# Attention turned by DMA in fp16 halves instead of by TensorE, with the query projection moved into gate/up, in a fused attention and FFN kernel

## The reference

```
xn = layernorm(x)                                   # x: 8 x 1024 x 256
q = elu(xn @ Wq.T) + 1;  k = elu(xn @ Wk.T) + 1;  v = xn @ Wv.T     # 16 heads of 16
kv_state = sum over tokens of k (x) v;  k_state = sum of k          # per batch and head
attn = (q . kv_state) / max(q . k_state, 1e-6)
local = conv over 3 tokens, per channel, of xn, + conv_b
out = x + (attn + local) @ Wp.T + bp + (silu(xn @ wg.T) * (xn @ wu.T)) @ wd.T   # hidden 768
```

## Time and profile before

| | |
|---|---|
| median of 3 runs | 507.55 us (507.19 to 507.74) |
| the profiled execution: its own time | 506.9 us |
| its span, first to last instruction | 505.3 us |
| TensorE matmul busy | 491.4 us, 97% |
| VectorE / ScalarE / GpSimd busy | 430.5 us, 85% / 334.3 us, 66% / 144.7 us, 29% |
| granted TensorE clock | 0.999 of full speed |

### The profile page before, as it was taken

How to read it: one execution, slowest core, us unless ns; L and a number is a source line. 1 busy time by engine, 2 the same in 40 slices (tenths; PEclk the granted TensorE clock), 3 DMA queues, 4 the chain that set the end, 5 groups by cost and what they waited for, 6 DMA issues and landing times.

```text
span 505.3 us, 11017 instructions
## 1 busy us (share of the span) xinstructions
PE 491.4 (97%) x3968; PEld 306.1 (61%) x3968; DVE 430.5 (85%) x833; ACT 334.3 (66%) x522; POOL 144.7 (29%) x152
## 2 busy tenths in 40 slices
PE   7888999999999999999999999999999999999997
PEld 6545364755747566474756657475565756657576
DVE  4889898889888898988889888889888889897786
ACT  2676866667485775757667485667758576674770
POOL 3563415140321405033140502314041141401050
PEclk9999999999999999999999999999999999999999
DMA  8573434333524423252352325233342442233012
GB/s 307 183 91 77 86 82 87 68 111 51 151 43 111 99 45 125 41 166 42 83 125 42 125 42 164 43 82 100 54 138 42 126 82 42 87 50 74 3 42 84
DMA packets 68653, 45.36 MB, mean 90 GB/s; under 512 B 33424, under 2 KB 68112, under 8 KB 68624
## 3 DMA queue, kind: packets, MB, share of 16 engines
q1 hardware_dynamic: 59360, 35.79, 25.2%
q0 software_dynamic: 8448, 8.39, 11.0%
q10 hardware_dynamic: 816, 0.79, 0.5%
HBM read 20.32 MB, written 8.39 MB: 57 GB/s over the span
## 4 chain that ended last, share of the span: by engine, by line
PE 88%; DVE 5%; ACT 3%; DMA 2%; issue 1%; ACTq 0%; DVEq 0%
PE ps L1202 16%; PE ps L1039 16%; PE ps L1211 15%; PE ps L1221 15%; PE ps L1145 15%; PE ps L1101 5%; PE ps L1110 3%; PE ps L1164 2%; DMA wv_raw<-in_L_attn_Wv_dram 2%; DVE maxima L665 1%; DVE hl L902 1%; DVE hid L896 1%; ACT hh L544 1%; DVE cb L764 0%; PE ps L1085 0%
## 5 line engine op out<-in xcount | busy, mean ns | idle before, releaser
L536 ACT ACTIVATE act_g<-ps,scales 128x512 f32<-128x512 f32 x96 | 65.9, 687 | 42.0 <-PE ps L1211 39.7
L896 DVE SCALAR_TENSOR_TENSOR hid<-act_g,scales,ps 128x512 f32<-128x512 f32 x96 | 71.4, 744 | 21.2 <-ACT act_g L536 20.7
L902 DVE TENSOR_TENSOR hl<-hid,hh 128x512 f16<-128x512 f32 x96 | 66.3, 691 | 1.8 <-ACT hh L544 0.4
L361 POOL TENSOR_TENSOR xT<-xh,xl 128x1024 f32<-128x1024 f16 x15 | 32.3, 2153 | 109.4 <-issue 109.4
L544 ACT ACTIVATE hh<-hid 128x512 f16<-128x512 f32 x96 | 59.7, 622 | 5.3 <-DVE hid L896 5.3
L1202 PE MATMUL ps<-xh,g_wh 128*128 128x512 f16 x192 | 57.6, 382 | 2.1 <-ACT u_wh L455 1.4
L1211 PE MATMUL ps<-xl,g_wh 128*128 128x512 f16 x192 | 57.1, 379 | 0.0
L1202 PE MATMUL ps<-xh,u_wh 128*128 128x512 f16 x192 | 57.1, 379 | 0.0
L1211 PE MATMUL ps<-xl,u_wh 128*128 128x512 f16 x192 | 57.1, 379 | 0.0
L1221 PE MATMUL ps<-d_wh,hh 128*128 128x256 f16 x384 | 52.4, 273 | 2.2 <-DVE hid L896 2.2
L499 ACT ACTIVATE k_neg<-ps,scales 128x512 f32<-128x512 f32 x30 | 20.6, 687 | 49.4 <-PE ps L1145 49.4
(11 more groups left out here) (149 smaller groups left out, 965.5 us busy)
## 6 DMA issues: line engine op xcount, KB each, us to landing
xb<-bp_sb SPq DMA_DIRECT2D x16, 512.0 KB, 3.4
xb<-in_L_attn_x_dram POOLq DMA_DIRECT2D x16, 512.0 KB, 5.9
x_in<-in_L_attn_x_dram SPq DMA_DIRECT2D x15, 512.0 KB, 4.1
out_dram<-out_sb SPq DMA_DIRECT2D x14, 512.0 KB, 2.9
out_dram<-out_sb SPq DMA_DIRECT2D x4, 256.0 KB, 2.1
wg_int<-in_L_ffn_w_gate_dram SPq DMA_DIRECT2D x1, 768.0 KB, 7.1
wu_int<-in_L_ffn_w_up_dram SPq DMA_DIRECT2D x1, 768.0 KB, 8.6
wd_int<-in_L_ffn_w_down_dram SPq DMA_DIRECT2D x1, 768.0 KB, 11.1
```

The source lines that it names most:

```text
L536: nc.scalar.activation(act_g[:, j % 2, :], ps[:, gate_bank(j), :], ACT.Silu, scale=silu_in).then_inc(silu_ready, 1)
L896: nc.vector.scalar_tensor_tensor(out=hid[:, j % 2, :], in0=act_g[:, j % 2, :], scalar=h_mul, in1=ps[:, gate_bank(j) + 1, :], op0=ALU.mult, ...
L902: nc.vector.tensor_tensor(hl[:, j, :], hid[:, j % 2, :], hh[:, j, :], ALU.subtract).then_inc(hl_ready, 1)
```

## The change

1. `transpose_attn` is gone from the 14 steps that attend (it stays for the last batch in step (7, 1)). Instead ScalarE writes `attn_h` (fp16, `attn_high(p)`), VectorE writes the rest, `attn_l` (`attn_low(p)`), SP turns each with one DMA transpose (`turn_attn`), GpSimd adds the two into `y` (`begin_y(p)`), and VectorE adds `local` to it (`put_y(p)`, now with both inputs in SBUF).
2. `project_q` moves behind `gate_up(2)`, with `accumulate(1)` behind it, and has banks 4 and 5 for itself; ScalarE evicts both of its parts (`query_evict`, after `silu(2)`; VectorE's `relu_q` is gone), and its exponential (`query_exp`) and `put_q` run in the *next* step.
3. `project_kv(1)` stands before `query`; `project_y(0)` behind `gate_up(5)` and `project_y(1)` between `down(0)` and `down(1)`.
4. On VectorE `stats` comes before the first taps, the second taps go into gate/up, `x_high`/`x_low` move from j = 4 to j = 2, `put_y` to j = 2 and 3, `y_high` to j = 3 and 4, `y_low(0)` to j = 4, `y_low(1)` behind `hidden_low(5)`.
5. In the last step everything of item 1 applies to the attention of batch 6, and `query_evict` and `query_exp` stand before the first `silu`.

The diff, cut to its core:

```
@@ SP
             def turn_attn(b, c):
+                turn([(attn_h, aT_h, attn_h_ready, ah_turned), (attn_l, aT_l, attn_l_ready, al_turned)],
+                     at(b, c, 2, 2), lambda channels: channels[:, :, :, :])
@@ GpSimd
+            def begin_y(b, c, p):
+                pool.wait_ge(ah_turned, at(b, c, 16, 16))
+                pool.wait_ge(al_turned, at(b, c, 16, 16))
+                nc.gpsimd.tensor_tensor(y[:, :, cols].rearrange("p k (i t) -> p i k t", i=2), aT_h[:, tiles, :, :],
+                                        aT_l[:, tiles, :, :], ALU.add).then_inc(y_begun, 1)
...
                     layernorm(nb, ncx)
+                if attend:
+                    begin_y(b - 1, c, 0)
+                    begin_y(b - 1, c, 1)
@@ ScalarE, step
+                    query_exp(*((b, 0) if c == 1 else (b - 1, 1)))
                 key_parts(0)
+                if not ahead:
+                    attn_high(b - 1, c, 0)
                 key_parts(1)
-                if past:
-                    query_parts()
+                if attend and ahead:
+                    attn_high(b - 1, c, 0)
+                if not ahead:
+                    attn_high(b - 1, c, 1)
+                    query_evict()
+                    query_exp(b, c)
@@ VectorE, step
+                if ahead:
+                    stats(nb, ncx)
                 tap(pb, pc, 0, 0)
                 tap(pb, pc, 1, 0)
+                put_q(pb, pc)
+                put_k(0)
...
                         hidden(j)
+                        if attend and j == 0:
+                            attn_low(b - 1, c, 1)
+                        if attend and j == 1:
+                            tap(pb, pc, 0, 2)
+                            tap(pb, pc, 1, 2)
                         if j >= 1:
                             hidden_low(j - 1)
-                        if attend and j == Y_SPLIT[0]:
+                        if attend and j == 4:
                             y_low(b - 1, c, 0)
+                        if attend and j in (2, 3):
+                            put_y(b - 1, c, j - 2)
@@ TensorE, step
+                    project_kv(1)
+                    query(b - 1, c, 0, QKV)
+                    query(b - 1, c, 1, QKV)
+                    gate_up(0)
+                    accumulate(0)
+                    gate_up(1)
...
+                        if j == Q_SPLIT:
+                            project_q()
+                            accumulate(1)
+                    project_y(b - 1, c, 0, WP)
                     down(0, DOWN)
+                    project_y(b - 1, c, 1, WP)
                     down(1, DOWN)
```

More of the change, by code:

```diff
@@ L481, in outer_tap, with attn_high @@
                                      scale=cw[:, k, 2 * side:2 * side + 1]).then_inc(tap_scaled, 1)
+            def attn_high(b, c, p):
+                act.wait_ge(attn_ready, at(b, c, 2, p + 1))
+                if p == 0 and not (isinstance(b, int) and b == 0 and c == 0):
+                    act.wait_ge(ah_turned, at(b, c, 16, 0))
+                tiles = slice(2 * p, 2 * p + 2)
+                nc.scalar.activation(attn_h[:, tiles, :], attn[:, tiles, :], ACT.Copy,
+                                     scale=attn_to_y).then_inc(attn_h_ready, 1)
             def y_high(b, c, p):
@@ L559, in step @@
                     silu(j)
+                    if attend and ahead and j == 0:
+                        attn_high(b - 1, c, 1)
                     if j == 2 and past and not attend:
@@ L563, in step @@
                         hidden_high(j - 1)
+                    if past and ahead and j == (X_SPLIT if attend else FIRST_X_SPLIT):
+                        x_high(*((b, 1) if c == 0 else (b + 1, 0)))
+                    if past and ahead and j == Q_SPLIT:
+                        query_evict()
                     if j in (0, 1) and not past:
@@ L980, in step @@
                     hidden_low(J - 1)
+                    if attend:
+                        y_low(b - 1, c, 1)
                     put_state()
@@ L1001, in step @@
                     hidden_low(2)
[L1002 removed]
+                    put_q(b, c)
                     hidden(4)
@@ L1280, in step @@
                 project_kv(0)
-                if attend:
-                    pe.wait_ge(res_ready, at(b, c - 1, 2, 2))
-                    pe.wait_ge(acc_kept, at(b, c, 1, 0))
+                if not attend:
+                    project_kv(1)
[4 more added lines that the diff above has]
+                    gate_up(1)
+                    for j in range(2, J):
+                        gate_up(j)
+                    pe.wait_ge(hid_ready, at(b, c, J, J - 1))
+                    down(0, DOWN)
+                    pe.wait_ge(res_ready, at(b, c - 1, 2, 2))
+                    down(1, DOWN)
+                    return
+                pe.wait_ge(res_ready, at(b, c - 1, 2, 2))
+                pe.wait_ge(acc_kept, at(b, c, 1, 0))
+                pe.wait_ge(q_read, at(b, c - 1, 1, 1))
+                if not ahead:
                     query(b - 1, c, 0, QKV)
                     query(b - 1, c, 1, QKV)
-                project_kv(1)
-                project_q()
-                accumulate(0)
-                if attend:
-                    transpose_attn(b - 1, c, 0, TURNED)
-                    transpose_attn(b - 1, c, 1, TURNED)
-                accumulate(1)
-                gate_up(0)
-                gate_up(1)
+                    project_kv(1)
+                    project_q()
+                    accumulate(0)
+                    accumulate(1)
+                    gate_up(0)
+                    gate_up(1)
+                else:
+                    project_kv(1)
+                    query(b - 1, c, 0, QKV)
+                    query(b - 1, c, 1, QKV)
+                    gate_up(0)
+                    accumulate(0)
+                    gate_up(1)
                 if isinstance(b, int) and b == 1 and c == 0:
```

167 lines of the change are left out of this document (88 added, 79 removed).

## The result

The changed kernel takes 548.91 us (median of 4 runs, 546.63 to 551.33), against 507.61 us for the kernel before on the same chip: ratio 1.082, 95% interval 1.080 to 1.084. Forecast were 558.0 us, with 520 to 572 as range. The profiled execution took 551.33 us, the slowest of the four, at a granted TensorE clock of 0.984; its span is 549.7 us.

The account below looks back on a forecast made before the run. TensorE, busy 97% of the span, was taken to bound the kernel. A step of 33.0 us against 29.83 gives 41 us in 13 steps, plus 9 for the last: about 558 us, range 520 to 572.

Parts of the forecast that it names:

- What bounds, and what is removed: TensorE, busy 97%, sets the end; removing the transposes saves 1.03 us in each of 14 steps, 14.4 us.
- Term 1: gate_up(0) waits for the values of the second 256 tokens: +0.2 us a step, bounds 0.1 and 0.3.
- Term 2: accumulate(0) waits for the second normalise, as GpSimd's rstd blocks VectorE: +1.2 us a step, bounds 0.1 and 1.5.
- VectorE always first: Lower bound of the wait at accumulate(0): VectorE starts ahead of GpSimd's instruction, leaving 0.1 us.
- Term 3: gate_up(5) waits because GpSimd's adds of the attention halves block VectorE: +0.4 us a step, bounds 0 and 1.1.
- Term 4: project_y(0) waits for y_low(0): 1.2 us bare chain plus 1.2 for put_xT's block, +2.4 a step, bounds 1.1 and 3.2.
- Sum of a loop step: 28.80 us plus the waits, 33.0 us a step against 29.83: +3.2, in 13 steps 41 us.
- long adds block only in part: Rival: either put_xT or rstd blocks, not both; 31.3 to 32.3 us a step, 527 to 548 us; chance 0.25.
- Term 5: In the last step the first y projection starts at 25.9 us instead of 16.7: +9 us, bounds 5 and 11.
- Edges: The first two steps change little, taken as 0 within 1 us; the following steps cost +3.2 us each.
- the favoured case, with all blocks: The forecast's own case, GpSimd's adds blocking VectorE throughout: 548 to 572 us; chance 0.45.
- taken at its word: The skill page's rule, each collision costing all the rest, raises put_xT's 1.2 to 2.0 us, the forecast by 10.

Follow-up runs that it names:

- experiment 1: The kernel before, with both attention transposes done twice on TensorE in the 14 steps that have them: 519.52 us, ratio 1.0245.
- Experiment 3: The changed kernel with GpSimd's add of the attention halves cut to one column, the low attention half left out of y: 537.32 us, ratio 1.0568.
- experiments 4 and 9 to 12: 4: changed kernel, X_SPLIT 4 instead of 2, 531.96 us; 10 and 12: experiment 9's kernel, split of x last, 547.99 us, or moved into gaps, 522.2 us.
- Experiment 2: The changed kernel with y_low of feature half 0 moved from j = 4 to j = 3: 531.48 us, ratio 1.0481.
- experiment 7: The changed kernel with 27 unused fp32 matmuls in TensorE's idle time before the last step's first y projection: 547.48 us, ratio 1.0767.
- experiment 5: The changed kernel with attn_low(1) ahead of hidden(0) in the last step only: 548.34 us, ratio 1.081.
- experiment 9: The changed kernel with y_low of half 0 earlier, the split of x back at block 4 and the last step reordered: 522.0 us, ratio 1.029.
- experiment 11: Experiment 9's kernel with x_low cut to 128x2 elements in the steps that also attend: 514.2 us, ratio 1.0135.

## Why the prediction was right, and where its numbers were off

The direction, and the place of the largest loss, were right: TensorE pays for each VectorE instruction behind which the y projection is queued. Point by point, by the terms of the prediction.

- **What bounds, and what is removed.** TensorE did set the end (experiment 1). The 1.03 us of a step hold: the step at 235.46 takes 31.71 us against 29.83, and its new gaps are 0.22 + 0.09 + 0.09 + 1.06 + 1.42 = 2.88; less 1.03 that is 1.85, and 1.88 were measured. Experiment 1's 0.89 is what a second set adds.
- **Term 1** (+0.2): measured 0.22 (the query's rows end at 242.48, gate_up(0) starts at 242.70).
- **Term 2** (+1.2) is the step that failed in kind: there is no wait for the attention, only 0.09 us ahead of the sums (244.44 to 244.53), as there were behind `project_q` in the kernel before, and 0.09 more ahead of `gate_up(2)`. VectorE's taps came first (238.65, against 238.82 for `rstd`), kept their 1.41 us, and GpSimd was the one that was stretched. The bound "VectorE always first" was the case. The block is real, but who is stretched is decided by 0.2 us.
- **Term 3** (+0.4): 1.06 measured (block end 255.09, next start 256.15), near its upper bound. Experiment 3 shows that it is GpSimd's add: without it `x_low` takes 1.28 us and the wait is gone.
- **Term 4** (+2.4): 1.42 measured, the bare chain, for which 1.2 was worked out. The 1.2 for the copy of x did not come in the loop. Term 3's block delayed `x_low` by 1.9 us, but it did not hang on this: in experiment 3 `x_low` is free, and the copy still begins 6.5 us behind the issue of its transpose. What failed is the 3.1 us taken from the earlier trace rows for the landing. It took 6.4, so the copy met `state`, where nothing waits; after 3.1 it would have begun at about 258.2, beside `hidden_low(3)` and `y_low(0)` (an estimate). Where it landed within 3.2 us, in the second step with attention and the last but one, the block did come: `put_y` and the low half took 2.61 and 2.10 us instead of 0.68, with waits of 3.19 and 2.68 for `yl`. The landing goes with the order of the DMAs: 6.4 us where the transpose is issued 0.7 us behind the DMA into `xb`, 3.1 to 3.2 where it is issued ahead of it or over 5 us behind it (experiments 4 and 9 to 12). That this DMA is what slows it was not tried by itself. Experiment 2 shows that the chain's 1.42 us are all of the wait for `yl` in the loop.
- **Sum of a loop step:** 28.80 + 0.22 + 0.09 + 0.09 + 1.06 + 1.42 = 31.7, measured 31.71; predicted 33.0. So the rival "long adds block only in part" describes the loop (31.3 to 32.3 a step). Its 527 to 548 us do not follow from its own terms: +1.5 to +2.5 us in 13 steps and 9 for the last give 536 to 549, which holds the measured 548.9. Nor do the bounds of terms 2 to 4 give the forecast's 548 to 572; they give 521 to 581, and 548 and 572 are where the rivals begin.
- **Term 5** (+9): 11.9 measured. The projection started 9.0 us later after the step's start (25.67 against 16.72), as worked out (25.9); the remaining 2.9 us are the half clock behind the idle, which the prediction had nowhere (experiment 7).
- **Edges** (0 for the first two steps, 3.2 for each of the next): the head gave +1.1, the first attention step +2.4, the second +5.7, the last but one +5.2. In the two large ones the copy's block costs 1.4 to 1.9 us of waiting, and the half clock behind it some 1.7: 4 us at 0.58, and 8 us at 0.90 and 0.67, in the rows above.

Together 1.09 + 2.44 + 5.65 + 18.2 + 5.16 + 11.87 = 44.4 us of span (549.7 − 505.3). The errors went both ways: too much for blocks in the loop (1.3 x 10 = 13), too little for the edges and the clock. That the time lies among those of the favoured case, with all blocks, is luck: some 6 us of it are the half clock, which no term had (2.9 + 1.7 + 1.7 in the profiled run, 0.012 of 547 us in the two middle ones), and without them it is 542 to 543, inside the rival's times.

The page of the Trainium skill that the prediction weighed (SBUF — State Buffer, "Who interferes with whom") is borne out: `x_low` beside the add (3.21 us), the low half beside the copy (2.10) and, in experiment 5, the taps beside the add (3.15) are such rows. What the rule doesn't give is when each comes up, and on that, above all on the landing of the transpose, the 10 us of the estimate hung: "taken at its word" it would have given 568, further off.

No version beat the kernel before. The best complete one (experiment 9) is at 1.029; in a loop step of it VectorE's last third holds TensorE up, and ScalarE's SiLU comes next (experiment 11). Each turned half costs these two and GpSimd a subtraction, a cast and an add that the transposes did not; that this is what fills them was not tried by itself.

What stays open: whether the low half of x could be made in the 1.05 us that VectorE stands still ahead of `put_y` in experiment 9, and what slows its transpose. The 1.1 us of the head need not come from the change: in the experiments on the changed kernel, whose head is the same code, it ends at 43.73 to 44.64 us, against 44.56 here and 43.47 in the kernel before.

The half clock's share differs between executions. The runs of a kernel whose profile shows the full clock throughout lie within 1.0 us, those of the changed kernel within 4.7, and the granted clock goes with them: 0.991, 0.988, 0.988 and 0.984 for 546.63, 548.40, 549.42 and 551.33 us; in experiment 7, 1.000 for the run of 544.73 us and 0.994 for the three of 547.33 to 548.21. What is missing to the full clock, times the span, is 4.9 us in the fastest run of the changed kernel and 8.8 in the slowest (an estimate), so it explains 3.9 of the 4.7. Why the clock falls in one execution and not in another is not shown.

## What to carry to other kernels

When work leaves the engine that sets the end, write down what it will wait for next, instruction by instruction: here 1.0 us a step was saved and 2.9 us of waits came in, 1.4 of them from one instruction standing one block too late. Such repairs do not add up; after two of them the next engine is the bound, and its busy time between two deadlines, not over the span, says how much is left. And price an idle gap with what follows it: some us without a matmul also cost the clock behind them. Take the time that a DMA needs from issue to landing from the place where it will run: this one had 3.1 us in its old place and 6.4 in its new one.
